# One fetch of source keys for two node tiles of a graph network

## What is computed

```
h   = relu(layernorm(x))
m   = silu(silu(LN([h[src], edge_attr] @ W1 + b1)) @ W2 + b2)      # one message per edge
agg = segment_sum(m, dst)                                          # layer 0
x   = x + LN(silu([agg, h] @ Wu + bu))
h   = relu(layernorm(x))
agg = segment_sum(h[src], dst)                                     # layer 1
x   = x + relu((h + agg) @ M1 + c1) @ M2 + c2
```

## Time and profile before

| | us |
|---|---|
| median of 3 runs (5370.26 to 5372.14) | 5370.95 |
| the profiled execution, its own time | 5364.65 |
| its span, first to last instruction | 5362.9 |
| POOL busy | 3721.5 |
| PE busy | 3760.8 |
| DVE busy | 3427.9 |
| ACT busy | 2145.2 |

### The profile page before, as it was taken

How to read it: one execution, slowest core, us unless ns; L and a number is a source line. 1 busy time by engine, 2 the same in 40 slices (tenths; PEclk the granted TensorE clock), 3 DMA queues, 4 the chain that set the end, 5 groups by cost and what they waited for, 6 DMA issues and landing times. The chain is left out here.

```text
span 5362.9 us, 73932 instructions
## 1 busy us (share of the span) xinstructions
PE 3760.8 (70%) x24431; PEld 2852.1 (53%) x24431; DVE 3427.9 (64%) x5403; ACT 2145.2 (40%) x3187; POOL 3721.5 (69%) x3907
## 2 busy tenths in 40 slices
PE   5556666666666666666666666666666768999997
PEld 4434444444444444444444444444444547999994
DVE  5467777777777777777777777777777681111111
ACT  1135445544444444454444444544544530000003
POOL 2777777777777777777777777777777206777770
PEclk9568788888888888888888888878888858999999
DMA  3123333333333333333333333333333227999992
GB/s 98 49 82 106 104 104 109 106 104 100 111 104 104 103 105 104 104 109 106 104 101 108 106 104 102 107 103 104 110 105 104 82 62 300 352 354 352 351 354 59
DMA packets 361303, 729.02 MB, mean 136 GB/s; under 512 B 156402, under 2 KB 206834, under 8 KB 350306
## 3 DMA queue, kind: packets, MB, share of 16 engines
q1 hardware_dynamic: 238338, 598.51, 30.4%
q0 software_dynamic: 122592, 125.78, 11.8%
HBM read 450.70 MB, written 273.27 MB: 135 GB/s over the span
## 5 line engine op out<-in xcount | busy, mean ns | idle before, releaser
L730 POOL DMA_INDIRECT gat<-layer_rows,idx x3752 | 3548.2, 946 | 1145.3 <-issue 1142.0
L1063 ACT ACTIVATE node_buffers<-ps 128x800 bf16<-128x800 f32 x1264 | 1058.0, 837 | 1966.0 <-PE ps L986 1947.4
L775 PE MATMUL ps<-one_hots,edge_buffers 128*128 128x80 f32 x3128 | 576.4, 345 | 849.0 <-DVE cT L822 847.4
L1187 DVE TENSOR_TENSOR node_buffers<-ps,node_buffers 128x1600 bf16<-128x1600 f32 x632 | 1146.6, 1814 | 0.0
L775 PEld LDWEIGHTS ps<-one_hots,edge_buffers 128*128 128x128 f32 x3128 | 521.2, 252 | 998.7 <-issue 993.0
L986 PE MATMUL ps<-node_buffers 128*128 128x200 bf16 x5056 | 726.0, 272 | 243.8 <-ACT node_buffers L1063 128.2
L986 PEld LDWEIGHTS ps<-node_buffers 128*128 128x128 bf16 x5056 | 467.7, 106 | 651.8 <-issue 510.9
L1137 DVE TENSOR_TENSOR edge_buffers<-ps,gat 128x512 f32<-128x512 f32 x391 | 269.8, 690 | 808.7 <-issue 685.7
L1185 DVE TENSOR_TENSOR node_buffers<-ps,node_buffers 128x1024 bf16<-128x1024 f32 x632 | 770.7, 1219 | 9.6 <-issue 0.7
L1664 PE MATMUL ps<-edge_buffers,node_buffers 125*128 125x192 bf16 x7900 | 686.3, 248 | 6.1 <-PEq L1400 6.1
L1664 PEld LDWEIGHTS ps<-edge_buffers,node_buffers 125*128 125x128 bf16 x7900 | 665.7, 139 | 19.8 <-issue 19.8
(11 more groups left out here) (186 smaller groups left out, 3197.4 us busy)
## 6 DMA issues: line engine op xcount, KB each, us to landing
stored_counts<-node_buffers SPq DMA_DIRECT2D x632, 400.0 KB
node_buffers<-stored_counts SPq DMA_DIRECT2D x79, 3200.0 KB
gat<-layer_rows,idx POOLq DMA_INDIRECT x3752
edge_buffers<-in_edge_quads SPq DMA_DIRECT2D x391, 128.0 KB, 3.1
node_buffers<-in_x SPq DMA_DIRECT2D x5, 625.0 KB
layer_rows<-node_buffers SPq DMA_DIRECT2D x25, 125.0 KB
residual_rows<-node_buffers SPq DMA_DIRECT2D x5, 625.0 KB
layer_rows<-node_buffers SPq DMA_DIRECT2D x5, 625.0 KB
```

Of the source, the lines that this page charges most:

```text
L730: pool.indirect_dma_start(out=gat[:, j, c, :], out_offset=None, in_=table[:, :], in_offset=bass.IndirectOffsetOnAxis(ap=idx[:, half, j, c: ...
L775: mm = pe.matmul(to[:, 0:2 * WIN], rows_of[:, 2 * k:2 * k + 2, :].rearrange("p c f -> p (c f)"), oh[:, j, 2 * k:2 * k + 2, :].rearrange("p ...
L1063: a.activation(stage[:, u % STAGES, part * GP * T:(part + 1) * GP * T].rearrange("p (b k) -> p b k", b=2), ps[:, 2:4, 0:4 * T], ACT.Copy). ...
L1187: v.tensor_tensor(high_hot[:, u % PAIR_SLOTS, :, :], per_tile(high_numbers, GP), bcast(high_key[:, b % 2, at], 2 * T), ALU.is_equal).then_ ...
```

## The change

One indirect DMA now serves two tiles, `2d` and `2d + 1`. A partition stands for two neighbouring nodes (partitions 0 to 63 for tile `2d`, 64 to 127 for tile `2d + 1`), and its row holds 128 keys (512 bytes) that begin at the first edge of the first of the two: since the edges are sorted, the keys of the second follow those of the first. `SLOTS` goes from 64 to 128. There are `DUOS = 40` such pairs.

- Ahead of layer 0's rounds, PE picks the offsets and degrees of even and odd nodes with 6 small f32 products against `ident` (`select_pairs`), and DVE copies them out and adds the two degrees (3 instructions). PE waits for the copy (`c_pair`) ahead of its rounds, POOL ahead of its first fetch of keys.
- `FETCH` goes from 0 to 1, and only even tiles have a fetch and a mask.
- The mask is 3 DVE instructions for 128 slots: slots from the first node's degree on get `T + 1` added to the high key (the number that tells the second node), and slots past the sum of both degrees are set to 0.
- `turn_keys` has 2 products to a tile in place of 4, with 128 columns of weights in place of 64; the second `activation` of `copy_keys` has no bias any more.
- In the setup `shift` goes, two small `memset` come, and the offsets stay f32 in `off`.

```diff
-    SLOTS = 64
+    SLOTS = 128
+    DUOS = -(-TILES // 2)
...
-                v.tensor_scalar(shift[:, :], number_i[:, :], 64.0, float(T + 1), ALU.is_ge, ALU.mult).then_inc(s_const, 1)
+                v.memset(deg[:, NT:T0 + 2 * DUOS], 0.0)
+                v.memset(off[:, NT:T0 + 2 * DUOS], 0.0).then_inc(s_const, 1)
...
-        FETCH, MASK, KEYS_TURN, HOTS, COUNT, STORE = 0, 4, 6, 8, 9, 13
+        FETCH, MASK, KEYS_TURN, HOTS, COUNT, STORE = 1, 4, 6, 8, 9, 13
...
                     b = tile_at(e, j, FETCH)
-                    if b is not None:
-
-                        wait(pool, c_kt, b - 1)
+                    if b is not None and b % 2 == 0:
+                        d = b // 2
+
+                        wait(pool, c_pair, 1)
+                        wait(pool, c_kt, 2 * (d - 1))
                         wait_alone(pool, "gpsimd")
                         pool.indirect_dma_start(
-                            out=node_keys[:, b % 2, :, :].rearrange("p k e -> p (k e)").bitcast(f32), out_offset=None,
+                            out=node_keys[:, d % 2, :, :].rearrange("p k e -> p (k e)").bitcast(f32), out_offset=None,
                             in_=ktab.unsqueeze(1),
-                            in_offset=bass.IndirectOffsetOnAxis(ap=off_i[:, T0 + b:T0 + b + 1], axis=0)).then_inc(c_gat[b % 2], 16)
+                            in_offset=bass.IndirectOffsetOnAxis(ap=pair_off[:, d:d + 1], axis=0)).then_inc(c_gat[d % 2], 16)
...
+                def select_pairs():
+
+                    for k, (of, parity) in enumerate(((off, 0), (deg, 0), (deg, 1))):
+                        for h in range(2):
+                            mm = pe.matmul(tp[0][h * 64:(h + 1) * 64, k * DUOS:(k + 1) * DUOS], ident[:, parity:128:2],
+                                           of[:, T0 + h:T0 + h + 2 * DUOS - 1:2], start=True, stop=True)
+                    mm.then_inc(c_sel, 1)
+
                 def turn_keys(b):
 
-                    wait(pe, c_msk, b + 1)
+                    wait(pe, c_msk, b // 2 + 2)
                     wait(pe, c_copy, 2 * units_before(tile_step[b] + KEYS_TURN - COUNT + 1))
                     wait(pe, c_kc, 2 * b)
+                    half = slice(b % 2 * 64, b % 2 * 64 + 64)
                     for k in range(2):
-                        for h in range(2):
-                            mm = pe.matmul(tp[k][h * 64:(h + 1) * 64, 4 * T:4 * T + 64], node_keys[:, b % 2, :, k],
-                                           identb[:, h:128:2], start=True, stop=True)
+                        mm = pe.matmul(tp[k][:, 4 * T:4 * T + 64], node_keys[:, b // 2 % 2, :, k], identb[:, half], start=True, stop=True)
                     mm.then_inc(c_kt, 1)
...
                     for j in range(EARLY):
                         edges(0, j)
+                    select_pairs()
+                    wait(pe, c_pair, 1)
                     rounds(step, WSUM)
...
-                    a.activation(high_key[:, b % 2, :], tp[1][:, 4 * T:4 * T + 64], ACT.Identity, bias=shift[:, :]).then_inc(c_kc, 1)
+                    a.activation(high_key[:, b % 2, :], tp[1][:, 4 * T:4 * T + 64], ACT.Copy).then_inc(c_kc, 1)
...
+                def mask(d):
+
+                    wait(v, c_gat[d % 2], 16 * (d // 2 + 1))
+                    wait(v, c_msk, d + 1)
+                    slots = iol[:, 0:SLOTS, 0]
+                    v.tensor_scalar(slot_second[:, :], slots, pair_deg[:, 0, d:d + 1], float(T + 1),
+                                    ALU.is_ge, ALU.mult).then_inc(c_test, 1)
+                    wait(v, c_test, 2 * d + 2)
+                    high = node_keys[:, d % 2, :, 1]
+                    v.tensor_tensor(high, high, slot_second[:, :], ALU.add).then_inc(c_test, 1)
+                    wait(v, c_test, 2 * d + 3)
+                    v.scalar_tensor_tensor(high, slots, pair_deg[:, 1, d:d + 1], high, ALU.is_lt, ALU.mult).then_inc(c_msk, 1)
...
                     b = tile_at(e, j, MASK)
-                    if b is not None:
-                        mask(b)
+                    if b is not None and b % 2 == 0:
+                        mask(b // 2)
...
+                    v.wait_ge(c_sel, 1)
+                    v.tensor_copy(pair_deg[:, :, :], tp[0][:, DUOS:3 * DUOS].rearrange("p (k d) -> p k d", k=2)).then_inc(c_test, 1)
+                    v.tensor_copy(pair_off[:, :], tp[0][:, 0:DUOS]).then_inc(c_pair, 1)
+                    v.wait_ge(c_test, 1)
+                    v.tensor_tensor(pair_deg[:, 1, :], pair_deg[:, 0, :], pair_deg[:, 1, :], ALU.add).then_inc(c_msk, 1)
```

More of the change, by code:

```diff
@@ L109, in build_gnn @@
         number_i = sb("number_i", [128, 1], i32)
-        shift = sb("shift", [128, 1])
         one_col = sb("one_col", [128, 1], bf16)
@@ L116, in build_gnn @@
         identb = sb("identb", [128, 128], bf16)
-        off_i = sb("off_i", [128, NT], i32)
-        deg = sb("deg", [128, NT])
+        off = sb("off", [128, T0 + 2 * DUOS])
+        deg = sb("deg", [128, T0 + 2 * DUOS])
+        pair_off = sb("pair_off", [128, DUOS], i32)
+        pair_deg = sb("pair_deg", [128, 2, DUOS])
         w1n = sb("w1n", [128, F])
@@ L183, in build_gnn @@
         high_key = view([128, 2, 64], bf16)
-        slot_used = view([128, SLOTS], bf16)
+        slot_second = view([128, SLOTS], bf16)
         again(XB)
@@ L587, in _ @@
                 v.wait_ge(s_hist, HEAD * KC // HQ)
-                v.tensor_copy(deg[:, :], zp[0][:, 0:NT]).then_inc(s_deg, 1)
+                v.tensor_copy(deg[:, 0:NT], zp[0][:, 0:NT]).then_inc(s_deg, 1)
                 v.wait_ge(s_deg, 1)
-                v.tensor_reduce(worst[:, 4:5], deg[:, :], X, ALU.max).then_inc(s_test, 1)
+                v.tensor_reduce(worst[:, 4:5], deg[:, 0:NT], X, ALU.max).then_inc(s_test, 1)
                 v.wait_ge(s_tot, 1)
@@ L595, in _ @@
                 v.wait_ge(s_test, 6)
-                for k, least in ((1, HEAD), (3, WIN), (4, SLOTS + 1)):
+                for k, least in ((1, HEAD), (3, WIN), (4, SLOTS // 2 + 1)):
                     v.tensor_scalar(worst[:, k:k + 1], worst[:, k:k + 1], 1.0 - least, None, ALU.add).then_inc(s_test, 1)
@@ L601, in _ @@
                 v.wait_ge(s_tot, 2)
-                v.tensor_copy(off_i[:, :], ag[1][:, 0:NT]).then_inc(s_deg, 1)
+                v.tensor_copy(off[:, 0:NT], ag[1][:, 0:NT]).then_inc(s_deg, 1)
                 v.wait_ge(s_wt, 1)
@@ L717, in _ @@
                 pe.wait_ge(s_deg, 1)
-                pe.matmul(zp[1][0:NT, 0:1], deg[:, :], onesm[:, 0:1], start=True, stop=True).then_inc(s_tot, 1)
-                pe.matmul(ag[1][:, 0:NT], tri[:, :], deg[:, :], start=True, stop=False)
+                pe.matmul(zp[1][0:NT, 0:1], deg[:, 0:NT], onesm[:, 0:1], start=True, stop=True).then_inc(s_tot, 1)
+                pe.matmul(ag[1][:, 0:NT], tri[:, :], deg[:, 0:NT], start=True, stop=False)
                 pe.matmul(zp[0][:, 0:2 * F], ones[:, :], rows[:, 2:4, :].rearrange("o k f -> o (k f)"),
@@ L875, in build_gnn @@
         c_gat = [sem(f"stored_node_edges_gathered{k}") for k in range(2)]
+        c_sel = sem("pair_offsets_selected")
+        c_pair = sem("pair_offsets_ready")
         c_test = sem("stored_slots_compared")
```

## The result

The changed kernel takes 5324.39 us in the median (5318.17 to 5325.56, 4 runs) against 5371.34 for the kernel before (5370.26 to 5372.14, 4 runs): a ratio of 0.991, 95% interval 0.9893 to 0.9928. It is faster by 47.0 us, and the forecast was 48.7. The profiled execution took 5318.17 us, 46.5 less than the one before. In the later runs both are some 6 us quicker, and the difference is the same within the spread: 5317.97 us (5313.32 to 5319.12, 5 runs) against 5365.53, ratio 0.9911 (0.9898 to 0.9925).

The account below looks back on a forecast made before the run. The prediction took POOL's never-waiting, never-empty queue of indirect DMAs in layer 0 as the bound. 39 places of 1.248 us are 48.7 us, all other terms count 0, so 5370.95 - 48.7 = 5322.3 us, range 5316 to 5334.

Parts of the forecast that it names:

- POOL's row is the bound; 39 places of 1.248 us leave it: POOL's queue in layer 0: 79 fetches become 40, each one place, so 48.7 us less.
- 512 bytes cost what 256 did: POOL's fetch of keys: the wider fetch still costs one place of 1.248 us, busy for 0.944 us.
- The page's figure of bytes over 436 GB/s: Fetch of keys: 32 KB more are 0.075 us each; if POOL carried them, 3.0 us for 40, leaving 45.7.
- rival D: DVE's new mask on SBUF holds up POOL's descriptors: at most 12 us, so 5334 us; chance 0.04.
- counted in rows: POOL's indirect DMAs: the preparing work goes by rows, which stay 128, so a wider fetch costs no more.
- DVE's mask: DVE in layer 0: 3 instructions per pair, 36 us in all against 35.6, covered by 1.8 us to spare per block.
- PE and ACT at 0: Beside POOL's row: PE's 316 small products (20.2 us) become 158, ACT does 6.7 us less; both count 0.
- The start: Start of layer 0: the offsets are ready before POOL asks at 209.0, so nothing waits; uncovered, a few us once.
- The setup: below 0.2 us: Setup: one DVE instruction is swapped for two tiny ones, costing below 0.2 us.
- likeliest case: The forecast itself, a fetch costs one place in POOL's queue: 5322 us, own range 5317 to 5328; chance 0.83.
- E: POOL holds each of 40 fetches until its rows land: 3.74 us each, 150 against 98.6, so 5422 us; chance 0.03.
- rival B: POOL's cost of a fetch grows with its bytes, up to twice: anything from 5322 to 5372 us; chance 0.07.

Follow-up runs that it names:

- extra_fetch: The changed kernel with one more unread indirect DMA of 128 rows of 512 bytes at each of the 39 odd tiles: 5365.12 us.
- two_fetches: The changed kernel with only the first 2 of the 40 fetches of keys, later masks and turns working on stale keys: 5269.46 us.
- wide_before: The kernel before with its 79 fetches bringing 512 bytes to a partition in place of 256, only the first 64 keys used: 5364.14 us, ratio 0.9999.
- masks_x4: The changed kernel with DVE's three mask instructions issued three times more for each pair, on tiles that nothing reads: 5319.28 us.
- prices: The changed kernel with 39 more unread indirect DMAs, 13 each of 64 rows and 16 rows of 512 bytes and 128 rows of 1536 bytes: 5362.15 us.
- fetch_at_0: The changed kernel with the fetch of keys back at step 0 of its tile, ahead of the first gather: 5322.72 us (10 runs).
- before_3: The kernel before with no edit, its third profile, on another chip: 5363.85 us.
- after_3: The changed kernel with no edit, its third profile, on another chip: 5316.66 us.

## Why the prediction was right, step by step

- **POOL's row is the bound; 39 places of 1.248 us leave it.** Right, and shown from both sides: putting 39 back gives all of it back (`extra_fetch`), taking 38 more out gives 47.3 to 47.8 us more in the stretch (`two_fetches`). Forecast 48.7, measured 48.0 to 48.6 between three profiles of each kernel.
- **512 bytes cost what 256 did.** Right in size: 0.944 us both. The page's figure of bytes over 436 GB/s (the Trainium skill, "DMA: Bandwidth & Descriptors", Anatomy of one DMA) would, as an estimate and if POOL had to carry them, have made 0.075 us per fetch, and 6 us in `wide_before`; the measured 2.4 us of stretch is below it.
- **The 0.1 to 0.7 us that the stretch lacks of 48.7.** The sum gave the mask no price on POOL. The first profile after has 0.67 us more in lengthened indirect DMAs than the one before (0.85 against 0.18, see `masks_x4`), which is nearly the 0.7 it lacks: rival D is there, but at under 1 us, not 12. The prediction had looked for it in POOL's gaps, where it does not show, and three of the four lengthened places of the kernel before stand beside its mask too.
- **Why they cost the same.** My reason, that POOL's work is "counted in rows", is wrong. `prices` shows that it is counted in instructions: 16 rows cost 0.853 us and 128 cost 0.944. The conclusion stood because the change kept 128 rows; for a change in the number of rows it would have misled.
- **DVE's mask.** Forecast 36 us in all, measured 39.2 (0.309, 0.306 and 0.365 us, 40 of each), hidden as forecast. DVE's idle time ahead of the gathered rows from 2000 to 2400 us went from 70.7 to 64.2 us, so the spare 1.8 us a block became 1.6.

```profile
L1197 DVE SCALAR_TENSOR_TENSOR node_buffers<-iol,pair_deg,node_buffers 128x128 bf16<-128x128 bf16 x40 | 14.6, 365 | 1.4
L1191 DVE TENSOR_SCALAR node_buffers<-iol,pair_deg 128x128 bf16<-128x128 bf16 x40 | 12.4, 309 | 0.0
L1195 DVE TENSOR_TENSOR node_buffers<-node_buffers 128x128 bf16<-128x128 bf16 x40 | 12.2, 306 | 1.4
```

- **PE and ACT at 0.** Right: the products went from 20.2 to 17.5 us, the copies lost 7.1 us, and none of it shows in the time.
- **The start.** Right that it is hidden, and the bounds were far too high. I had bounded six products at 5.8 us; they began at 203.93 and ended at 204.79, 0.9 us in all, and the offsets were there at 205.2, 5.9 us before POOL asked for them (211.06). `fetch_at_0` shows what the cover is worth: 5.3 us.
- **The setup: below 0.2 us.** The two tiny instructions cost 0.06 us each, but the setup as a whole was 2.07 us longer in the profile after. This, with -1.4 at the end of layer 0 and +0.8 behind it, is why the span moved by 46.5 and not by the 48.0 of the stretch. My own range for the likeliest case had room for it, and the sum had no term for it.
- **E, POOL held until landing.** Out: rows landed 2.6 us after the issue and POOL went on after 1.25.
- **Readings that do not hold as written.** 0.478 us is the mean of the two products of that row, not the most (the longer one took 0.535). POOL's idle time in layer 0 was not all "issue": four gaps of 0.3 us, 1.2 in all, are put down to PE, but they are no longer than the others. For rival B, 40 fetches at twice 1.248 are 99.8 us, not 99.9. None of these moves the forecast.

## What to carry to other kernels

Where a queue never waits and is never empty, count its instructions, not its bytes or busy time: here an indirect DMA costs 1.15 us of POOL's row where it brings 8 KB and 1.25 where it brings 192 KB, and the way to speed is fewer, fuller ones. Check for real slack on the engines behind it by looking at what they wait for, and prove the bound by adding the work back and by taking more away. When a step is taken off the path, ask what has to be ready for the first use in its new form: a wait at the head of the queue is the one place where nothing covers it.

## What was not expected of the hardware

**A fixed price.** An indirect DMA of 16 rows keeps POOL busy for 0.853 us, one of 128 rows for 0.944, and the 0.3 us between two of them stay whatever the shape. I had put the place of one of 16 rows, gap included, at some 0.5 us; it is 1.15.

**The clock of TensorE in the last stage.** The profiled execution of `fetch_at_0` was 5366.76 us, 44 above its median, though its stretch (3954.42 us) and its layer 1 were like the others'. Its windows (layer 1, then the last products in two parts) show where it went:

```profile
4400.00:5200.00 800.00, 790.02 (x8887) 767.65 (x8886) 82.47 (x309) 41.20 (x152) 596.31 (x624) 0.99 0.91 347
5200.00:5310.00 110.00, 92.02 (x351) 45.47 (x351) 14.02 (x36) 30.20 (x48) 0.00 (x0) 0.59 0.20 45
5310.00:5365.00 55.00, 42.55 (x164) 19.34 (x162) 7.94 (x19) 17.54 (x28) 0.00 (x0) 0.72 0.12 28
```

The same stages in the second profile of the changed kernel:

```profile
4397.00:5200.00 803.00, 793.27 (x8918) 770.63 (x8917) 82.56 (x310) 41.20 (x152) 595.34 (x624) 0.99 0.90 345
5200.00:5262.00 62.00, 47.31 (x276) 24.17 (x274) 10.93 (x28) 23.80 (x40) 0.00 (x0) 0.97 0.33 75
5262.00:5316.00 54.00, 38.67 (x208) 18.88 (x204) 10.45 (x25) 22.05 (x37) 0.00 (x0) 0.97 0.15 34
```

A closer window of `fetch_at_0` shows that 0.59 and 0.72 are means over a change of level:

```profile
5230.00:5340.00 110.00, 93.55 (x262) 41.08 (x260) 13.37 (x32) 31.84 (x50) 0.00 (x0) 0.50 0.16 37
```

After 800 us in which PE was busy for 790 at a granted clock of 0.99, the clock fell to 0.50, the lower of its two levels (1.2 of 2.4 GHz), for some 110 us in the one execution, with PE busy for 93.55 of them, and stayed at 0.97 in the other. From the first of the last products to the end it took 151.8 us in the one and 106.2 in the other. Two executions of `extra_fetch` (5404 and 5424 us) and two more of `fetch_at_0` (5348 and 5378) are long as well, with mean clocks of 0.824 to 0.836 where the others of these two have 0.838 to 0.849; they have no trace, so that it is the same drop is not shown. The mean clock does not tell the long ones by itself: an execution of the kernel before has 0.828 at 5368.03 us. What starts the drop is open.

**The setup is not repeatable.** POOL's and DVE's steps there run side by side and the same instruction takes different times: one `tensor_scalar` of 128x625 on POOL, in one place of the program, took 1.78 us in the first profile before and 3.01 in the first one after.

```profile
156.39 1.78 POOL L430 TENSOR_SCALAR node_buffers<-node_buffers 128x625 f32<-128x625 f32 x1
```

```profile
156.86 1.77 DVE L485 TENSOR_TENSOR node_buffers<-node_buffers,stat 125x1280 f32<-125x1280 f32 x1
157.27 3.01 POOL L432 TENSOR_SCALAR node_buffers<-node_buffers 128x625 f32<-128x625 f32 x1
```

It is not the change that does this. Seven of the 13 profiles have 1.8 us there and six have 3.0, and each kernel has both: the kernel before 3.02 in `before_3`, the changed one 1.78 in `after_3`. Where it is the short one, POOL's first issue comes at 197.7 to 199.8 us (leaving out `fetch_at_0`, which waits for the offsets), where it is the long one at 199.5 to 203.1. In the long case shown it starts beside a large DVE instruction that is itself longer (1.77 us, against 1.49 in the first profile before). A low clock of TensorE is not what makes the setup long: from 160 to 180 us the granted clock is 1.00 in the four profiles with the latest first issue (201.6 to 203.1) and 0.50 in the other nine. What decides between the cases was not tried apart.
